# x turned by the DMA as 16-bit halves instead of by TensorE, x chunks projected ahead of B and C, the x transposes first on the load queue, and VectorE joining all four chunks

## What is computed

```python
proj = jnp.einsum('bld,pd->blp', hidden_states, in_proj_w)
gate = proj[..., :I]
hbc = proj[..., I:I + CONV_DIM]              # x, B and C before the convolution
for k in range(K):                           # K = 4 taps along the sequence
    conv = conv + pad[:, k:k + L, :] * conv_weight[:, k]
xBC = jax.nn.silu(conv)
dtx = dt_p[..., None] * x
def step(state, inp):
    state = state * dA_t[..., None, None] + dtx_t[..., None] * B_t[:, :, None, :]
    y_t = jnp.einsum('bhpn,bhn->bhp', state, C_t)
y = jnp.moveaxis(ys, 0, 1) + x * D[None, None, :, None]
yn = (yg * lax.rsqrt(var + EPS)).reshape(B, L, I) * norm_weight
yn = yn * jax.nn.silu(gate)
out = jnp.einsum('bli,di->bld', yn, out_proj_w)
```

## Time and profile before

| what | value |
|---|---|
| three runs | 3263.53 to 3265.32 us, median 3264.49 us |
| the profiled execution | 3263.63 us; its span from first to last instruction 3261.7 us |
| TensorE busy in the span | 3238.3 us (99%) |
| VectorE busy | 2566.5 us (79%) |
| ScalarE busy | 1809.8 us (55%) |
| GpSimd busy | 1016.0 us (31%) |
| one block in the middle | 44.87 us |

### The profile page before, as it was taken

The page is one execution under the profiler, slowest core; times in us unless marked ns, Lnnn a source line. Parts: engine busy times, 40 slices in busy tenths (PEclk is TensorE's granted clock), DMA queues, the critical chain, the costliest instruction groups (busy, mean ns, idle before and its releaser), DMA issues. The chain is left out here.

```text
span 3261.7 us, 86522 instructions
## 1 busy us (share of the span) xinstructions
PE 3238.3 (99%) x32858; PEld 2691.5 (83%) x32858; DVE 2566.5 (79%) x4255; ACT 1809.8 (55%) x3274; POOL 1016.0 (31%) x740
## 2 busy tenths in 40 slices
PE   8999999999999999999999999999999999999999
PEld 6788888888888888888888888888888888888888
DVE  6788888888888888888888888888888888887443
ACT  5566555666556665556665566655566655554111
POOL 1134332233332333322333323333223322122333
PEclk9999999999999999999999999999999999999999
DMA  8443464445544464346444464446444542224321
GB/s 273 164 142 128 154 216 139 142 135 187 174 129 141 154 200 152 129 143 200 150 146 144 146 192 154 129 154 208 133 141 138 184 148 103 78 102 147 101 84 58
DMA packets 322030, 484.59 MB, mean 149 GB/s; under 512 B 152958, under 2 KB 198430, under 8 KB 312524
## 3 DMA queue, kind: packets, MB, share of 16 engines
q1 hardware_dynamic: 320604, 483.08, 46.2%
q0 software_dynamic: 368, 0.85, 0.1%
q10 hardware_dynamic: 1024, 0.27, 0.0%
HBM read 310.01 MB, written 144.75 MB: 139 GB/s over the span
## 5 line engine op out<-in xcount | busy, mean ns | idle before, releaser
L1210 PE MATMUL low_banks<-ht,wt 128*128 128x512 f32 x6144 | 1419.4, 390 | 0.8 <-DVE xc L1460 0.8
L1210 PEld LDWEIGHTS low_banks<-ht,wt 128*128 128x128 f32 x6144 | 1153.0, 188 | 246.7 <-DVE xc L1460 1.2
L1460 DVE SCALAR_TENSOR_TENSOR xc<-low_banks,cvw,xc 128x496 f32<-128x496 f32 (+2 forms) x1152 | 824.4, 718 | 217.2 <-ACT xc L1345 190.0
L1303 PE MATMUL bank<-wot,gy 128*128 128x512 f32 x3072 | 727.0, 392 | 0.0
L1303 PEld LDWEIGHTS bank<-wot,gy 128*128 128x128 f32 x3072 | 571.9, 188 | 119.6
L1141 POOL TENSOR_TENSOR r<-rv,neg_half 128x4 f32<-128x4 f32 x64 | 97.3, 1520 | 1701.9 <-DVE rv L1540 1701.9
L1345 ACT ACTIVATE xc<-low_banks,cvb,cvw 128x512 f32<-128x512 f32 x384 | 299.5, 780 | 490.1 <-PE low_banks L1210 490.1
L1210 PE MATMUL bank<-ht,wt 128*128 128x512 f32 x1536 | 388.5, 402 | 0.0
L1210 PEld LDWEIGHTS bank<-ht,wt 128*128 128x128 f32 x1536 | 280.3, 189 | 56.8
L1122 POOL TENSOR_TENSOR segr<-adts,mask_le 128x1024 fp32r<-128x1024 f32 x128 | 242.9, 1918 | 200.5 <-DVE adts L1451 200.5
L1324 ACT ACTIVATE xc<-xc 128x512 f32<-128x512 f32 x384 | 234.5, 625 | 38.0 <-DVE xc L1460 37.3
(11 more groups left out here) (195 smaller groups left out, 3721.6 us busy)
## 6 DMA issues: line engine op xcount, KB each, us to landing
ht<-h_d SPq DMA_DIRECT2D x63, 2048.0 KB, 7.8
acc_d<-acc SPq DMA_DIRECT2D x64, 1024.0 KB, 4.3
acc<-acc_d SPq DMA_DIRECT2D x56, 1024.0 KB
wt_d<-wnext SPq DMA_DIRECT2D x98, 512.0 KB, 4.2
wt<-wt_d SPq DMA_DIRECT2D x70, 512.0 KB, 4.7
stage<-in_L_attn_in_proj_w SPq DMA_DIRECT2D x70, 256.0 KB, 2.7
wot<-wt_d SPq DMA_DIRECT2D x28, 512.0 KB, 6.6
xb<-in_x SPq DMA_DIRECT2D x8, 1024.0 KB, 7.6
```

The source lines that it names most:

```text
L1210: ins = pe.matmul(pb[:, :], wt[:, n, l, k, :], ht[:, rr, k, :], start=(q == 0), stop=(q == len(products) - 1))
L1303: ins = pe.matmul(bank[OUT[t]][:, :], gy[:, c, l, t * P:(t + 1) * P], wot[:, rr, c, :], start=(c == 0 and q == 0), stop=(c == CT - 1 and q ...
L1460: ins = dve.scalar_tensor_tensor(dst, src, cvw[:, n, TAPS - 1 - k:TAPS - k], dst, ALU.mult, ALU.add)
```

## The change

TensorE's 16 transposes and ScalarE's four copies out of PSUM are gone. In their place, for each x chunk `c`: ScalarE splits the chunk into 16-bit halves (`split`), SyncE issues a DMA transpose of them (`turn_x` is now SyncE's), and VectorE joins the turned halves to f32 (`join_x`). The scan reads `xturn` instead of `dtx`.

The chunks are renumbered so that x is 0 to 3, and B and C are 4 and 5. C times B on TensorE therefore waits for SiLU of chunks 4 and 5 now (`NCV * it + NCV`), where it waited for the first two.

On SyncE the four transposes stand ahead of `exchange()` and of everything else in the block; in the seven blocks with weight loads they stand between these. `turn_next` is moved behind the load of `h` for the next block, and `next_split` on ScalarE to the block's end. On VectorE `pair(3)` and `find_here` go behind the scan matrix, and `pair(5)` with two joins behind the chain that follows the scan.

```diff
-    first = ([2 * INNER + g * NS, 2 * INNER + GN + g * NS] + [INNER + g * GI + c * P for c in range(CT)]
+    first = ([INNER + g * GI + c * P for c in range(CT)] + [2 * INNER + g * NS, 2 * INNER + GN + g * NS]
              + [g * GI + c * P for c in range(CT)])
...
-    dtx = sb("dtx", [P, TT, GI])
+    xturn = sb("xturn", [P, CT, TT, P])
+    xhalf = nc.alloc_sbuf_tensor_at("xhalf", [P, CT, 2, BLK], U16, offset=gy_at + 8 * TT * HG * L)
+    thalf = [nc.alloc_sbuf_tensor_at(f"thalf{c}", [P, 2 * TT, P], U16,
+                                     offset=(gy_at, sh.segr_at + 8 * BLK)[c // 2] + 4 * BLK * (c % 2)) for c in range(CT)]
...
+        TURNS_AT = (2, 3, 4, 6)
+
+        def turn_x(it, c):
+
+            if c == 2:
+                sp.wait_ge(s_seg, SEGB * it + 2 * SEGB)
+                sp.sem_inc(s_xgo, 1)
+            sp.wait_ge(s_xsplit, CT * it + c + 1)
+            sp.sem_inc(s_xgo, 1)
+            sp.dma_start_transpose(thalf[c][:, :, :], xhalf[:, c, :, :].rearrange("p a n -> p (a n)")).then_inc(s_xdma[c], 16)
...
             if not turn:
+                for c in range(CT):
+                    turn_x(it, c)
                 exchange()
-                if not last:
-                    turn_next(it)
...
                 for n in range(NPJ - 1):
+                    if n in TURNS_AT:
+                        turn_x(it, TURNS_AT.index(n))
                     sp.wait_ge(s_proj, NPJ * it + n + 1)
...
-                    if n == NCV - 3:
+                    if n == TURNS_AT[-1]:
                         exchange()
-                    elif n == NCV - 1:
-                        turn_next(it)
...
+            if not last:
+                turn_next(it)
             if over:
...
-            def turn_x(t):
-
-                for c in range(CT):
-                    ins = pe.transpose(bank[XT[t]][:, c * P:(c + 1) * P], xc[:, 2 + c, t * P:(t + 1) * P], sh.ident[:, :])
-                ins.then_inc(s_xt, 1)
-
...
-                                            dtx[rows, t, h * HP:(h + 1) * HP], m[rows, t, h, :], start=True, stop=True)
+                                            xturn[rows, c, t, u * HP:(u + 1) * HP], m[rows, t, h, :], start=True, stop=True)
...
-            pe.wait_ge(s_silu, NCV * it + 2)
+            pe.wait_ge(s_silu, NCV * it + NCV)
...
-            pe.wait_ge(s_silu, NCV * it + NCV)
             pe.wait_ge(s_exp, SEGB * it + SEGB)
-            for t in range(TT):
-                turn_x(t)
-
-            pe.wait_ge(s_dtx, TT * it + 1)
...
-            pe.wait_ge(s_dtx, TT * it + TT)
+            pe.wait_ge(s_xjoin, CT * it + CT)
...
+            def split(c):
+                act.wait_ge(s_silu, NCV * it + c + 1)
+                act.activation(xhalf[:, c, :, :], xc[:, c, :].bitcast(U16).rearrange("p (n a) -> p a n", a=2),
+                               ACT.Copy).then_inc(s_xsplit, 1)
+
...
-            for n in range(1, NCV - 2):
+            for n in range(1, CT):
                 tap(n)
                 silu(n - 1)
+                split(n - 1)
...
-            tap(NCV - 2)
-            silu(NCV - 3)
-            tap(NCV - 1)
-            if prepare:
-                next_split(0)
-                next_split(1)
-            silu(NCV - 2)
-            silu(NCV - 1)
+            tap(CT)
+            silu(CT - 1)
+            tap(CT + 1)
+            split(CT - 1)
+            silu(CT)
+            silu(CT + 1)
             gate(0)
             gate(1)
-            for t in range(TT):
-                act.wait_ge(s_xt, TT * it + t + 1)
-                act.activation(dtx[:, t, :], bank[XT[t]][:, :], ACT.Copy).then_inc(s_dtx, 1)
+            act.wait_ge(s_xsplit, CT * it + CT)
...
             high(3)
             square(3)
+            if prepare:
+                next_split(0)
+                next_split(1)
...
+            def join_x(c):
+
+                dve.wait_ge(s_xdma[c], 16 * it + 16)
+                dve.tensor_copy(xturn[:, c, :, :].rearrange("p t n -> p (t n)").bitcast(U16).rearrange("p (n a) -> p a n", a=2),
+                                thalf[c][:, :, :].rearrange("p (a t) n -> p a (t n)", a=2)).then_inc(s_xjoin, 1)
...
                 ins.then_inc(s_conv, 1)
+                if n == CT - 1:
+                    join_x(0)
+                    join_x(1)
+                elif n == CT:
+                    join_x(2)
...
             for q in range(SEGB):
                 scan_matrix(q)
+            join_x(3)
+            pair(3, ld, 0)
+            find_here(0)
             join(1, la, lb, 5)
             join(1, lc, ld)
             pair(4, lb, 6)
-            pair(5, ld, 7)
-            join(2, la, lc)
-            join(1, lb, ld, 9)
...
             add_squares(3)
+            pair(5, ld, 7)
+            join(2, la, lc)
+            join(1, lb, ld, 9)
```

24 lines of the change are left out of this document (12 added, 12 removed).

## The result

The changed kernel takes 3278.33 us (median of 6 runs, 3276.54 to 3280.78), the kernel before 3263.8 beside it: the ratio is 1.0045, with an interval of 1.0033 to 1.0056. It is slower by 15 us, where 50 us faster was predicted. The profiled execution has a span of 3276.9 us.

The account below looks back on a forecast made before the run. TensorE was taken to bound the kernel before, and a circle through VectorE and ScalarE after, at 43.97 us per block. 64 x 0.90 = 57.6 less 7 gave 3214 us; range for 8 in 10, 3172 to 3283.

Parts of the forecast that it names:

- The circle, steps 1 to 4: Loop from scan through VectorE, ScalarE's taps, scan matrix and last join to the next scan: 43.97 us per block.
- Step 1: From the scan to the next block's first tap on VectorE: 23.95 us, before 22.44.
- The join's price: A 16-bit copy of 1024 elements on VectorE at two per cycle: 0.69 us, 0.61 from start to start.
- The landing: Last x transpose, issue to landing: 3.5 us, hidden within 3.8; with weight loads 4.75, costing 7 us over seven blocks.
- The moves on SyncE: Reordered transfers on SyncE's queue: counted at nothing, or 1 us in each of seven blocks if one is late.
- The sum: All 64 blocks 0.90 us shorter, 57.6 us, less 7 for late transposes, 50.6 us of gain: 3214 us.
- one-element joins: Rival: VectorE's joins run at one element per cycle, 1.22 us each; block 45.01, total 3281 us; chance 0.12.
- the transposes land late: Rival: x transposes land over 4.7 us after issue, each us more costing 64; at 5.8 us, 3334; chance 0.06.

Follow-up runs that it names:

- e5_spread: The changed kernel with one VectorE pair and one weight join moved from behind the chain into waits inside the output chain: 3267 us.
- e11_cbearly: The changed kernel with four matmuls of the second gate chunk put behind C times B on TensorE: 3269.7 us.
- e12: e5_spread and e11_cbearly together, with the third join behind the last taps and two pairs between the first taps: 3262 us.
- e18: e12 with both of those VectorE pairs put behind the taps of chunk 4: 3253.23 us.
- e16: e18 with ScalarE's tap of chunk 4 ahead of the exponentials, chunk 5's ahead of chunk 3's SiLU, and table loads brought forward: 3244.55 us.
- e19: e16 with the queue of e13_q_wotmid and one of the two pairs moved behind the second join: 3181.68 us, ratio 0.9747 to the kernel before.
- e1_queue: The changed kernel with the weight transposes of a group's last block issued behind the last weight chunk and the parameters: 3255.81 us.
- e13_q_wotmid: e1_queue with the four output weight loads issued in the next block, two behind the third x transpose, two behind the fourth; TensorE's wait moved too: 3239.10 us.
- e2_plainsum: The changed kernel with group 0's sum into the residual reading x without the stride, so its output differs: 3268.18 us.
- e4: The changed kernel with four useless matmuls of 512 columns added on TensorE ahead of the scan: gains 3.5 us.
- e6_lastbehind: The changed kernel with only the exchange issued ahead of the fourth x transpose: 3472.20 us.

## Why the prediction was wrong

**The balance.** Forecast were 58 us of gain in the blocks, less 7 for late transposes. Measured are 50 of gain, less 43 behind the group ends, 13 in group 0 and 8 in single blocks.

**The circle, steps 1 to 4: the size nearly right, the reason incomplete.** Counted from the scan at 1366.17: first taps at 23.56 (forecast 23.95), chunk 4's taps at 35.33 (35.71), last taps at 38.11 (38.46), scan matrix at 41.76 (41.97), scan at 44.07 (43.97). Step 1 was 0.4 too long, and the end 0.3 too short: from the start of the scan matrix to the scan I had 1.21 + 0.79 = 2.00, measured is 2.31. That these errors nearly cancel is luck. A steady block gains 0.79 us and not 0.90: 0.08 to 0.10 from the circle, the rest because the block of 44.87 was a little longer than most. TensorE's idle time ahead of the scan is 0.87 (forecast 0.8). The circle was only one of two paths of almost equal length, the other being TensorE's own order up to C times B: e5_spread and e11_cbearly each cut one and gained nothing in the steady block, and e12, e18, e16 and e19, which cut both, gained as far as the last taps came earlier. That did not make the forecast of this change wrong. It would have made wrong any forecast of a cure from the circle alone, as mine for e5 and e12 were.

**The join's price: right.** 0.73 to 0.75 us in the block, 754 ns on average, against 0.69 taken and 1.22 for the rival. So writing the two halves of the same 32-bit words did not hold the copy to one element per cycle.

**The landing: good enough, also in the seven blocks with weight loads.** The median is 3.0 us, 3.5 was taken. For the blocks with weight loads I took 4.75 us from issue to landing, 0.95 late, 7 us in all. Measured there are 5.1 us for one, and 0.7 us in four of the seven, under 3 us in all; it was the second transpose and not the last that was late. The 43 us lie one block further. In the block shown above the landing is 3.2 to 3.4; what is late is the issue, by 8.9 us.

**The step that failed is "The moves on SyncE".** It says that the weight transposes hold up the store of `acc`, the last weight chunk, the parameters and the output weights by 2 to 4 us, that "each has over 10 us until its use", and "I count these at nothing". The loads themselves had time. But I asked whether the loads would be late, and not what stands behind them in the queue: the x transposes of the next block, which the same change puts there and which VectorE's taps stand behind. These were issued up to 8.9 us late. The term was nothing, or 7 us if a load were late, and measured 43; moving transfers on SyncE's queue takes 19 of these away in e1_queue and 35 in e13_q_wotmid. The delay itself was sized at 2 to 4 us; in the block shown the store of `acc` is issued 29.1 us behind the scan, and 23.5 in the kernel before. Why a transpose is not issued until the transfers ahead of it have nearly landed stays open.

**Group 0 was not looked at.** The sum took 63 differences as equal. In group 0 four instructions are 0.39 us longer each, outside the critical work before and inside the circle after: 1.56 us in each of its blocks, about 10 us in all (e2_plainsum). The other 2 of its 13 us are one fall of the clock (the 47.25) and the block with weight loads (the 46.30). One row of groups in the profile before had shown it.

**The clock was not in the sum.** TensorE before never idled in a block; after it idles 0.87 us ahead of every scan, and some blocks, a few per run, then run a stretch at a granted clock of 0.50. Of the 8 us in single blocks, 1.5 for each of the three at 45.6 are of this kind. The blocks at 44.74, 0.7 over, are not: they have a late transpose, as shown, and occur in e1, e4 and e11 too.

None of the rivals was it. The time comes within 3 us of that of the one-element joins, 3281, but by chance: the joins took 0.75 us and not 1.22. The nearest in kind, "the transposes land late", had the right consequence, but was priced as a delay of every landing in every block and not as a hold in seven.

## What to carry to other kernels

When a transfer joins the path that sets the end, look through its queue one block further: everything that may still be moving when it is issued counts, above all loads that occur in one block of eight, where the mean shows nothing. When the binding engine's work is cut, work out all the other paths, not the first that fits, and go through the special blocks (first group, group ends) one by one, since slack that differed between them was invisible before. And fill the waits of VectorE with regard to GpSimd: where a piece stands decides whether it takes 0.54 or 1.53 us.

## What the runs showed of the hardware

- A DMA transpose behind 2.5 to 3 MB of plain transfers on the same queue came late: in one case (after) it is issued 8.9 us after its data are ready and lands in 3.3, in the other (e6_lastbehind) it is issued at once and lands after 6.3 instead of 3.0. Behind 1 or 1.5 MB (e6, groups 7 and 0) it landed within 3.3. Which of the two happens when is open.
- A DMA transpose of 128x1024 elements of 16 bits took 1.23 us to issue and 3.0 us to land where little else was under way (after, medians of 256).
- A 16-bit copy of 1024 elements on VectorE, writing every second 16-bit word, took 754 ns on average.
- TensorE's granted clock fell to 0.50 after idle times of 0.86 to 1.5 us ahead of the scan, in 1 to 3 of the blocks of groups 1 to 7 at 0.86, and in eight of these and all of group 0 at 1.5; each fall cost 1.5 us. Waits ahead of C times B, of 0.8 us in groups 1 to 7 and 1.2 to 1.4 in group 0 of e11_cbearly and e12_both, brought none.
- A one-input operation of VectorE on 512 elements took 1.53 us beside GpSimd's work (e12_both), 0.54 alone.
